# Loads of the output stage placed up to four strips later behind its stores, and a shorter chain of batch statistics

## What is computed

```python
# --- layer 0 ---
x = x + depthwise_conv_3x3(sign(group_norm(x)), sign(kernel))
# --- layer 1 (v = group_norm(x)) ---
ca_gate = sigmoid(fc(mean(v)) + fc(max(v)))          # one gain per image and channel
xc = v * ca_gate
m = mean(xc, channel)
y = scan_over_pixels(m)                              # a 16-state recurrence over H*W
s = conv_7x7([mean(xc, channel), max(xc, channel)])
x2 = xc * sigmoid(y) + xc * sigmoid(s)               # = xc * gate, one gate per pixel
mean, var = moments of x2 over batch and pixels      # one pair per channel
out = relu((x2 - mean) * rsqrt(var + eps) * gamma + beta)
x = x + out
```

## Time and profile before

| | |
|---|---|
| Median of 3 runs | 3325.71 us |
| Span of the profiled execution | 3373.7 us (no other time of it is given) |
| VectorE busy | 2976.3 us, 88% |
| ScalarE busy | 2701.0 us, 80% |
| TensorE busy | 2587.4 us, 77% |
| HBM read and written | 805.14 MB and 420.17 MB, 363 GB/s over the span |
| Output block, about | 2351 to 3374 us of the span |

### The profile page before, as it was taken

The page is one execution under the profiler, slowest core; times in us unless marked ns, Lnnn a source line. Parts: engine busy times, 40 slices in busy tenths (PEclk is TensorE's granted clock), DMA queues, the critical chain, the costliest instruction groups (busy, mean ns, idle before and its releaser), DMA issues. The chain is left out here.

```text
span 3373.7 us, 50742 instructions
## 1 busy us (share of the span) xinstructions
PE 2587.4 (77%) x17105; PEld 1657.5 (49%) x17105; DVE 2976.3 (88%) x4060; ACT 2701.0 (80%) x3772; POOL 56.8 (2%) x111
## 2 busy tenths in 40 slices
PE   7899999999999999999976333333776776766676
PEld 5566666666566666665432000000555555555555
DVE  8788999889998889988886999998999899888787
ACT  6788888888888888887763888887888888877777
POOL 3000000000000000000001100000000000000000
PEclk9999999999999999999986555555877778777767
DMA  8899999999999999998755999996999999999997
GB/s 318 328 374 399 386 367 366 364 368 401 374 364 365 369 398 384 366 367 335 274 129 122 380 420 419 420 421 261 382 428 430 428 426 420 415 386 374 373 369 289
DMA packets 199056, 1227.97 MB, mean 364 GB/s; under 512 B 29792, under 2 KB 38936, under 8 KB 157644
## 3 DMA queue, kind: packets, MB, share of 16 engines
q1 hardware_dynamic: 195884, 1223.41, 91.1%
q0 software_dynamic: 2976, 2.00, 0.3%
HBM read 805.14 MB, written 420.17 MB: 363 GB/s over the span
## 5 line engine op out<-in xcount | busy, mean ns | idle before, releaser
L1440 PE MATMUL psum<-signs,taps 128*128 128x448 f16 x4032 | 855.4, 355 | 29.4 <-DVE signs L1071 14.4
L1554 PE MATMUL psum<-signs,picked 12*128 12x448 bf16 x896 | 334.4, 517 | 340.4 <-DMA signs<-gate_scratch 276.6
L1945 ACT ACTIVATE stage<-psum 128x512 f32<-128x512 f32 x784 | 407.5, 614 | 209.1 <-DMA out_dram<-stage 186.7
L1440 PEld LDWEIGHTS psum<-signs,taps 128*128 128x128 f16 x4032 | 386.8, 98 | 351.7 <-issue 33.8
L1965 DVE SCALAR_TENSOR_TENSOR xc<-xt,curs,psum 128x1792 f32<-128x1792 f32 x222 | 452.0, 2077 | 121.7 <-PE psum L1554 119.2
L835 ACT ACTIVATE xt<-psum 128x896 f32<-128x896 f32 x416 | 378.0, 910 | 151.8 <-PE psum L1338 128.0
L1757 DVE SCALAR_TENSOR_TENSOR xc<-xt,curs,psum 128x1792 f32<-128x1792 f32 x224 | 455.8, 2077 | 34.0 <-PE psum L1554 33.1
L1691 ACT ACTIVATE xc<-xc 128x1792 f32<-128x1792 f32 x224 | 380.0, 1697 | 95.9 <-DVE xc L1757 95.9
L1122 DVE CUSTOM_DVE_ANT_0 xt<-scratch,xt 128x896 f32<-128x896 int8 x416 | 435.7, 1084 | 14.2 <-ACT scratch L843 14.2
L1338 PE MATMUL psum<-ident,stage 128*128 128x128 f32 x3066 | 410.2, 276 | 16.4 <-DMA stage<-x_dram 10.6
L1933 ACT ACTIVATE xc<-xc,bn,curs 128x1792 f32<-128x1792 f32 x224 | 411.1, 1899 | 7.6 <-DVE xc L1965 4.2
(11 more groups left out here) (222 smaller groups left out, 2830.4 us busy)
## 6 DMA issues: line engine op xcount, KB each, us to landing
xt<-x_scratch SPq DMA_DIRECT2D x210, 1792.0 KB
out_dram<-stage SPq DMA_DIRECT2D x112, 1792.0 KB, 13.6
stage<-x_dram SPq DMA_DIRECT2D x219, 896.0 KB, 9.0
xc<-x_scratch SPq DMA_DIRECT2D x210, 896.0 KB, 8.2
x_scratch<-xt SPq DMA_DIRECT2D x208, 896.0 KB, 8.5
x_scratch<-last_unit SPq DMA_DIRECT2D x16, 896.0 KB, 8.9
signs<-ssm_scratch SPq DMA_DIRECT2D x14, 448.0 KB, 4.6
xc<-ssm_scratch SPq DMA_DIRECT2D x14, 448.0 KB, 5.0
```

The source lines that it names most:

```text
L1440: return nc.tensor.matmul(turn[h % 2][:, b * 512:b * 512 + HB], taps[:, j, t, :], signs[:, j, r:r + RT // 2, dw:dw + W], start=t == 0, sto ...
L1554: last = nc.tensor.matmul(dst[:, b, :], picked[:, b * P:(b + 1) * P], gate_rows[:, s * BW:(s + 1) * BW], start=True, stop=True)
L1945: nc.scalar.activation(outs[n % 2][:, 2 * k:2 * k + 2, :].rearrange("p t c -> p (t c)"), out_ps[k % 4], ACT.Identity).then_inc(staged, 1)
```

## The change

Four things are edited.

1. SP's list in the output block is written out for all 112 strips. The gate of strip m+7 is still loaded when x2 of strip m is made, and now ahead of the slot. The slot load of strip f is issued in step f - 7 + behind(f), where behind(f) is 0 for strips up to 27, 1 from 28, 2 from 49, 3 from 70, 4 from 91. Gates get their own semaphores (`gates4`), which PE waits for, and VectorE waits for the slots (`arrived4`) before it makes u.
2. The chain of statistics is shorter: squares of the gains and the division by the count are made far ahead (`gains`, at the start of the statistics block), one multiplication takes the place of three, the Newton step takes three operations and not four, and one broadcast multiplication replaces two. `curs` for the first strip is copied in this block.
3. Of u of the first output strip, half 0 stays ahead of the chain; half 1 moves behind it.
4. On PE, in the first step alone, the transposes of strip 0 stand ahead of the gate of strip 2.

```diff
+        gains = pair_counts[:, :, :, :].rearrange("p j a k -> p (j a k)").rearrange("p (b k) -> p b k", k=2 * NJ)
...
                 for k in range(8):
                     delta_step(dve, 1, k)
+                nc.vector.tensor_scalar(gains[:, :, 0:NJ], par[:, :, NJ:2 * NJ], 1.0 / (NB * HW), None, ALU.mult
+                                        ).then_inc(gains_made, 1)
+                dve.wait_ge(gains_made, 1)
+                nc.vector.tensor_tensor(gains[:, :, NJ:2 * NJ], gains[:, :, 0:NJ], par[:, :, NJ:2 * NJ], ALU.mult
+                                        ).then_inc(gains_made, 1)
...
-                for j in range(NJ):
+                def first_strip(j):
                     nc.vector.scalar_tensor_tensor(
                         quarters(xc[0][:, j, :]), slot_quarters(0, j), curs[:, 1, j:j + 1],
                         gate_quarters(gate_ps3[0]), ALU.add, ALU.mult).then_inc(first_u, 1)
+                first_strip(0)
                 dve.wait_ge(squared3, NB * NS * NJ + Q3)
...
-                steps(nc.vector.tensor_tensor(wsum[:, :, 0:NJ], bnsum[:, :, 0:NJ], scales, ALU.mult))
-                steps(nc.vector.tensor_tensor(wsum[:, :, NJ:2 * NJ], bnsum[:, :, NJ:2 * NJ], scales, ALU.mult))
-                steps(nc.vector.tensor_tensor(wsum[:, :, NJ:2 * NJ], wsum[:, :, NJ:2 * NJ], scales, ALU.mult))
+                dve.wait_ge(gains_made, 2)
+                steps(nc.vector.tensor_tensor(wsum[:, :, :], bnsum[:, :, :], gains, ALU.mult))
...
-                steps(nc.vector.tensor_scalar(bn[:, 0:2, :], bn[:, 0:2, :], count, None, ALU.mult))
...
-                steps(nc.vector.tensor_tensor(t, t, rs, ALU.mult))
-                steps(nc.vector.tensor_scalar(t, t, -0.5, 1.5, ALU.mult, ALU.add))
-                steps(nc.vector.tensor_tensor(rs, rs, t, ALU.mult))
+                steps(nc.vector.scalar_tensor_tensor(t, t, -0.5, rs, ALU.mult, ALU.mult))
+                steps(nc.vector.scalar_tensor_tensor(rs, t, 1.5, rs, ALU.add, ALU.mult))
...
-                for j in range(NJ):
-                    steps(nc.vector.tensor_scalar(par[:, :, NJ + j], par[:, :, NJ + j], scale[:, j:j + 1],
-                                                  None, ALU.mult))
+                steps(nc.vector.tensor_tensor(par[:, :, NJ:2 * NJ], par[:, :, NJ:2 * NJ],
+                                              bn[:, 6:7, :].broadcast_to([P, NB, NJ]), ALU.mult))
+                nc.vector.tensor_copy(curs[:, 0:1, :], par[:, NB - 1:NB, :]).then_inc(cur_made4, 1)
+                first_strip(1)
...
+                def behind(m):
+                    return min((m - NS) * 5 // (total - NS), 4)
+                def fetch(m):
+                    sp.dma_start(slots[m % NS], x1_d[(m // NS - 2) % NB, :, 2 * (m % NS):2 * (m % NS) + 2, :, :]
+                                 ).then_inc(arrived4[m % NS], 16)
+                fetched = NS
+                for m in range(total):
+                    sp.wait_ge(x2_made, 2 * (m + 1) + X4)
+                    if m + NS < total:
+                        load_gate(sp, gates4, ((m + NS) // NS - 1) % NB, m % NS)
+                    while fetched < total and fetched - NS + behind(fetched) <= m:
+                        fetch(fetched)
+                        fetched += 1
+                    sp.wait_ge(staged, (m + 1) * TG + E4)
...
-                        if n + 2 < NN or more:
+                        first = isinstance(it, int) and it == 0 and n == 0
+                        if not first and (n + 2 < NN or more):
                             spread(it, n + 2)
                         pe.wait_ge(x2_made, it * (2 * NN) + 2 * (n + 1) + X4)
...
+                        if first:
+                            spread(it, n + 2)
...
                     dve.wait_ge(spread4, it * NN + n + 1)
+                    dve.wait_ge(arrived4[s], it * 32 + 16 * (n // NS + 1))
```

More of the change, by code:

```diff
@@ L1575, in binary_conv_then_gated_ssm_block @@
         bn = sb("bn", [P, 12, NJ])
+        assert 2 * NJ * NCNT == NB * 2 * NJ
+        gains = pair_counts[:, :, :, :].rearrange("p j a k -> p (j a k)").rearrange("p (b k) -> p b k", k=2 * NJ)
+        gains_made = sem("gains_made")
+        cur_made4 = sem("cur_made4")
         arrived3 = [sem(f"arrived3_{s}") for s in range(NS)]
@@ L1780, in _ @@
                 dve.wait_ge(reduced3, 4)
-                count = 1.0 / (NB * HW)
-                scales = par[:, :, NJ:2 * NJ]
-                steps(nc.vector.tensor_tensor(wsum[:, :, 0:NJ], bnsum[:, :, 0:NJ], scales, ALU.mult))
-                steps(nc.vector.tensor_tensor(wsum[:, :, NJ:2 * NJ], bnsum[:, :, NJ:2 * NJ], scales, ALU.mult))
-                steps(nc.vector.tensor_tensor(wsum[:, :, NJ:2 * NJ], wsum[:, :, NJ:2 * NJ], scales, ALU.mult))
+                dve.wait_ge(gains_made, 2)
+                steps(nc.vector.tensor_tensor(wsum[:, :, :], bnsum[:, :, :], gains, ALU.mult))
                 steps(nc.vector.tensor_reduce(bn[:, 0:2, :].rearrange("p a j -> p (a j)"),
@@ L1838, in binary_conv_then_gated_ssm_block @@
         arrived4 = [sem(f"arrived4_{s}") for s in range(NS)]
+        gates4 = [sem(f"gates4_{s}") for s in range(NS)]
         spread4 = sem("spread4")
-        cur_made4 = sem("cur_made4")
         u_made4 = sem("u_made4")
@@ L1866, in _ @@
                 for s in range(NS):
[L1867 to L1883, removed]
+                    sp.sem_inc(arrived4[s], 16)
+                    sp.sem_inc(gates4[s], 16)
+                total = NB * NS
+                def behind(m):
[12 more added lines that the diff above has]
+                    sp.wait_ge(staged, (m + 1) * TG + E4)
+                    sp.dma_start(out_strips[(m // NS - 2) % NB, m % NS * SP:(m % NS + 1) * SP, :].rearrange("(p t) c -> p t c", t=NT),
+                                 outs[m % 2][:, :, :]).then_inc(written[m % 2], 16)
                 for b in range(2):
@@ L1889, in spread @@
                 def spread(it, n):
-                    pe.wait_ge(arrived4[n % NS], it * 64 + 32 * (n // NS + 1))
+                    pe.wait_ge(gates4[n % NS], it * 32 + 16 * (n // NS + 1))
                     pe.wait_ge(u_made4, it * (2 * NN) + 2 * n)
@@ L1969, in _ @@
                 dve.sem_inc(x2_made, X4)
-                nc.vector.tensor_copy(curs[:, 0:1, :], par[:, bass.ds(place(0, 0), 1), :]).then_inc(cur_made4, 1)
                 dve.wait_ge(cur_made4, 1)
```

## The result

The changed kernel takes 3336.61 us (median of 5 runs, 3333.22 to 3343.62), the kernel before 3326.61 in the same comparison: a ratio of 1.0036, with a 95% interval from 1.0023 to 1.0048. It is slower by 10 us by the medians and by 12 by the ratio, where 7 us less were forecast, and the time lies above the stated range of 3312 to 3330.

A forecast was written before the change was run, and what follows sets the result against it. The DMA queue was taken to bound the output block's middle, VectorE and ScalarE its end. Terms -7.4 (lag) - 1.05 (chain) + 1.1 (transposes) + 0.4 (gains) = -6.95 us, from 3325.7 to 3318.8 us; range 3312 to 3330.

The forecast's parts named there:

- 0.7 + 6.9 + 0.1 + 8.02 = 15.7: it fits by 1.6 us: Output block at lag 4: issue, load, wake-up, u and x2 fit into two strips, 17.3 us.
- third rival: Output block at lag 4: loads become the wait, 6 to 28 us over 21 strips, put at 3338 us; chance 0.14.
- What bounds the kernel before: Middle of the output block: the queue binds at 8.67 us a strip, VectorE needs 8.02; timed runs keep 428 GB/s.
- first rival: Late output block: the slow 374 GB/s belongs to the timed runs too, -5.2 in all, 3320.5 us; chance 0.12.
- A missing load is worth 4.33 us: Output block: while the queue binds, each missing slot load brings all later work 4.33 us forward.
- fourth rival: Output block: VectorE, not the queue, sets the pace; missing loads bring nothing, -0.5, 3325.2 us; chance 0.09.
- The end: Last load's landing to the program's end: 49.0 us before, 24.3 after; the last load lands 17.3 later relative to stores.
- The chain of statistics: Statistics ahead of the output block: shorter chain and half a u moved behind it gain 1.05 us, bounds 0 and 1.9.
- Transposes ahead of the gate: First output strips: PE's new order makes u of strip 2 4.2 to 4.9 us late, costing 1.1 us (0.2 to 2.0).
- second rival: Start and end of the output block: first strips lose nothing, end overlaps better, -11, 3314.5 us; chance 0.13.
- from then on the queue stays full in both: After the second slot load: the queue stays full in both kernels, so the start's loss is up to 2.0 us.
- The signs it named: Output block: wrong if u waits for slots over 2 us a strip, or DMA share falls below 1 before the last strips.

The follow-up runs named there:

- lag 5: The changed kernel with lag 5 where it has lag 4 (strips from 91 on): median 3458.22 us.
- lag 4: The changed kernel's own strips from 91 on, and a run of the changed kernel with lag 4 from strip 28 on: median 3379.69 us.
- second profile: The kernel before, profiled once more with no edit: span 3320.3 us.
- half steps: Changed kernel with lag up to 3, PE's order of before, each lag step in two halves seven strips apart: median 3337.53 us, ratio 1.0039 to the kernel before.
- lag-3 kernel: The changed kernel with the lag held at 3 from strip 70 on: median 3321.29 us, ratio 0.9985 to the kernel before.

## Why the prediction was wrong

The sign was wrong, and it was decided by one step: "0.7 + 6.9 + 0.1 + 8.02 = 15.7: it fits by 1.6 us". The loop itself was right. Its parts add up to what was measured at lag 5 (15.1 against 15.2 us a strip) and at lag 4 (18.7 to 18.9 against 18.6 to 19). Wrong was the load's 6.9 us. The forecast read it from a transfer in a nearly empty queue, called it "at most", and put it into a queue that it held to be full. It is the time in an empty queue (6.7 at lag 5); at lag 4 a load takes 10.3 to 10.5 us, some 3.7 more, because the store that SP issued just before is still on its way. With 0.36 + 10.5 + 8.02 the loop is 18.9 and overruns the 17.3 by 1.6. The third rival named this mechanism, with 6 to 28 us of waits, and put the time at 3338 us; it had 0.14. From store 84 to 105 the changed kernel is 16.6 us over what the forecast had (12.3 + 4.3).

Point by point:

- **What bounds the kernel before:** right. The second profile has 8.7 us a strip, a full queue and no slow stretch, and its span is that of the timed runs, so the first rival is out.
- **A missing load is worth 4.33 us:** too much. Three steps gave 7.7 us, 2.6 each, so the fourth rival, by which they bring nothing, is out too. Behind the second and the third step the queue runs dry (behind the third the DMA share is 0.44 from 2912 to 2916; behind the first it stays at 0.94 or more). The stage of 4 us behind the second step in the changed kernel:

```profile
2724.00:2728.00 4.00, 3.31 (x25) 2.54 (x23) 3.96 (x3) 4.00 (x6) 0.00 (x0) 1.00 0.61 256
2728.00:2732.00 4.00, 0.62 (x5) 0.45 (x4) 4.00 (x4) 2.29 (x4) 0.00 (x0) 1.00 1.02 361
```

VectorE is busy throughout (3.96 and 4.00 of 4 us), and the rate is 256 and 361 GB/s. A likely reason, which no run shows by itself: the engines have 0.65 us to spare a strip, so they cannot use 4.33 us at once. The half steps, meant to keep the queue from running dry, gained nothing between stores 14 and 84, so what the rest of the 4.33 us goes to stays open.

- **The end:** right in mechanism. The last load of the changed kernel is issued at 3296.27 and lands 9.84 us later, and from the landing to the end it is 25.4 us (forecast 24.3); the rows answer to the earlier trace rows:

```profile
3296.27 9.84 DMA xt<-x_scratch
...
3306.20 4.07 DVE L1984 SCALAR_TENSOR_TENSOR xc<-xt,curs,psum 128x1792 f32<-128x1792 f32 x2 [1.45 <-DMA xt<-x_scratch]
3310.19 3.95 DVE L2002 TENSOR_TENSOR last_unit<-xc,xt 128x1792 f32<-128x1792 f32 x2
3314.06 3.95 DVE L2002 TENSOR_TENSOR signs<-xc,xt 128x1792 f32<-128x1792 f32 x2
```

- **The chain of statistics:** right, and somewhat better, 1.6 us instead of 1.05: from the last square to the first relu it is 8.74 us in five traces with the new chain and 10.37 to 10.38 in three with the old. The timeline of the changed kernel, for the earlier trace rows; the sums start 1.8 us after the last square starts, not 3.8:

```profile
2328.83 1.70 ACT L1695 ACTIVATE xc<-xc 128x1792 f32<-128x1792 f32 x1 [0.21 <-DVE xc L1766]
...
2330.65 1.08 DVE L1787 TENSOR_REDUCE bnsum<-scratch 128x16 f32<-128x112 f32 x4
...
2334.92 2.07 DVE L1778 SCALAR_TENSOR_TENSOR xc<-xt,curs,psum 128x1792 f32<-128x1792 f32 x1
...
2337.57 3.65 ACT L1951 ACTIVATE xc<-xc,bn,curs 128x1792 f32<-128x1792 f32 x2 [4.16 <-DVEq L1991]
```

- **Transposes ahead of the gate:** right in sign and in VectorE's delay, wrong in what it costs: 4.1 us instead of 1.1, and outside its bounds of 0.2 to 2.0. So the second rival, by which the start loses nothing, is out. The timeline of the changed kernel, for the earlier trace rows:

```profile
2343.49 3.42 PE L1926 MATMUL psum<-ident,last_unit 128*128 128x128 f32 x16 [4.24 <-DVE last_unit L2002]
...
2349.87 2.83 PE L1926 MATMUL psum<-ident,last_unit 128*128 128x128 f32 x12 [2.96 <-ACT stage L1963]
...
2353.36 0.37 SPq L1897 DMA_DIRECT2D out_dram<-stage  x1
2353.92 4.07 DVE L1984 SCALAR_TENSOR_TENSOR xc<-xt,curs,psum 128x1792 f32<-128x1792 f32 x2 [6.50 <-PE psum L1554]
...
2362.25 0.34 SPq L1885 DMA_DIRECT2D xt<-x_scratch  x1
...
2368.36 0.34 SPq L1897 DMA_DIRECT2D out_dram<-stage  x1
```

PE transposes four groups, then waits 2.96 us for ScalarE, and the gate comes last: VectorE idles 6.50 us, not 1.83. That is 4.7 us more, and 4.2 to 4.9 were forecast. The step that failed is "from then on the queue stays full in both". The second store follows the first by 15.0 us (8.4 with the gate first), and after the second load the queue is not full (the DMA share, next to last, is 0.79):

```profile
2368.00:2372.00 4.00, 2.53 (x14) 2.09 (x13) 3.87 (x3) 4.00 (x4) 0.00 (x0) 0.80 0.79 333
```

What stays is near VectorE's 4.7 us, not near the queue's loss at the second load.

- **The Trainium skill's rule** in DMA: Bandwidth & Descriptors, Rules for kernel authors ("Issue the DMA early, do compute, wait on its semaphore late"), which the forecast weighed against the trace, agrees with lag 4 and 5 here. At lag up to 3 the kernel is not slower for issuing late: with the gate first and the shorter chain the ratio is 0.9979. How much of that is the lag's no run shows, since none has the gate first, the shorter chain and no lag.

- **The signs it named:** of the two that it is wrong, one came clearly: the DMA share fell below 1 before the last strips (0.61 above). The waits of u for slots came to 1.7 us each (32.2 / 19), and the longest was 5.2, where under 1 was forecast.

The lag, forecast at -7.4 us, thus came to +11.4 against the second profile: -7.7 + 12.3 + 6.8.

## What to carry to other kernels

When a transfer is moved later, close the loop from its release back to its issue, and put into it the transfer's time in the queue as it will be there: the time in an empty queue can't be used beside the claim that the queue is full. Work that is left out of a full queue can be worth less than its transfer time: here 2.6 of 4.33 us. And what makes the first output early is of no use if the second waits for it: look at the next instruction of the engine whose wait moved.

## What was not expected of the hardware

One load of 1792 KB has four times from issue to landing in these traces, by what stands in the queue: 6.7 us at lag 5, 10.3 to 10.5 at lag 4, 17.0 in the full queue, and 19.9 late in the lag-3 kernel, where the reason is open. The busy share of the DMA engines hardly shows the difference: 0.98 with 386 GB/s against 1.01 with 423, so the GB/s are to be read, not the share.
